# Layer 2 of a two-layer convolution kernel: its 3x3 as four quarter-array matmuls per tap, its last convolution in float32 on row halves

## The chip, the cores and the metric

The kernel runs on one core of a Trainium2 chip. Its time is the device time of one execution, in microseconds (us). Engines: TensorE (PE in the rows, PEld for its weight loads), VectorE (DVE), ScalarE (ACT), GpSimd (POOL) and SyncE (SP), which issues most of the DMAs.

## What is computed

Input x is 4 images of 1024 channels, 64x64, float32. Layer 1 is a deformable bottleneck block; layer 2 is a masked block in four groups. Cut to what matters:

```python
# layer 1
out = relu(bn(conv1x1(x, w1)))                      # 1024 -> 256
offset = conv3x3(out, w_off) + b_off                # 256 -> 18
out = deform_conv3x3(out, offset, w2)               # 4 gathered corners per tap, 9 taps, 256 -> 256
out = relu(bn(out))
x = relu(bn(conv1x1(out, w3)) + x)                  # 256 -> 1024
# layer 2, everything in G=4 groups
m1 = expand(mask, 1024); m2 = expand(mask, 256)     # one 8x8 mask per group, each cell 8x8 pixels
out = relu(gconv1x1(x * m1, w1)) * m2               # per group 256 -> 64
out = relu(gconv3x3(out, w2, pad=1)) * m2           # per group 64 -> 64
out = gconv1x1(out, w3)                             # per group 64 -> 256
return relu(out + x)
```

## The kernel before

Work goes by blocks of 8 image rows (512 pixels, one PSUM bank wide); there are NB = 32 blocks, 8 per image. Every engine walks the same list of 42 steps, written out by hand, in program order, and waits on semaphores. In step s block s is in phase A (conv1, the pixel table in HBM), block s-1 in T (offsets, coordinates), block s-8 in B (deformable 3x3), block s-9 in C (conv3, layer 2's first convolution) and block s-10 in E (layer 2's 3x3 and last convolution). Steps 10 to 31 have all phases (22 steps); steps 32 to 39 have no A (8 steps); 40 and 41 drain. Steps go in pairs inside a hardware loop: `pipeline` takes two steps a turn.

A step is cut into nine taps k = 0 to 8. Per tap, GpSimd gathers four tiles of corners (`corners`, 8 slots), ScalarE scales the first corner (`corner0`), VectorE adds the other three in 12 operations (`interpolate`), TensorE transposes the sum (`turn_val`, 8 matmuls), ScalarE copies it out rounded (`valT_copy`), VectorE makes its remainder (`valT_low`), and TensorE multiplies one tap later (`tap(k-1)`, 12 float32r matmuls). `turn_val(k)` waits for `valT_low(k-1)`. Beside each tap stand other phases' pieces, in the table `beside` of each engine. For TensorE: `conv1`, `conv3`, `gconv1`, `offconv`, and at k = 6 `gconv2(0)`, at k = 7 `gconv2(1)` and `turn_offs`, at k = 8 `gconv3(0)`, `gconv3(1)` and a chunk of the next block's `conv1`; behind the last tap the other `gconv3`.

Layer 2 in detail. Two groups make a pair: one holds partitions 0 to 63, the other 64 to 127.

- `gconv1(pair)`: 256 channels in, 64 out, column halves of the array, into psR[pair].
- `ga_mask(pair)` (VectorE): one operation into `scratch`, then one per group (64 partitions each) into `ga`. `halo_ga`: six small copies between blocks' border rows.
- SyncE then copies each group's rows, shifted by one, to the other 64 partitions (`ga<-ga`, two DMAs of 264 KB), so that one matmul takes two vertical taps: `gconv2(pair)` needs 6 matmuls for 9 taps, per group, on a column half (128 rows by 64 columns).
- `gb_mask(pair)` writes `scratch`, ScalarE's `gb_hi` and VectorE's `gb_lo` split it into a float32r high part and a remainder, stacked on the partitions.
- `gconv3(m)`, m = 0 to 7: a 128-row matmul with `gw3_hi` and a 64-row one with `gw3_lo` into psR[m % 2]; VectorE's `out_add(m)` adds y; `gconv3(m)` waits for `out_add(m-2)`. Where phase A is off a float32 matmul with the identity adds y instead, and ScalarE's `out_relu` reads PSUM.
- The next step's `conv3(0)` and `conv3(1)` write the same two banks and wait for the last `out_add`s; `y_add(0)` must follow before `conv3(2)`. On VectorE there stand between them `coordinates` (16 small operations) and four of `interpolate`.

A plain float32 matmul shows as two records in the trace, a float32r one as one.

## Time and profile before

| | |
|---|---|
| median of three runs | 3182.59 us (3177.9 to 3191.78) |
| span of the profiled execution | 3179.8 us |
| TensorE busy | 2983.4 us, 94% |
| VectorE busy | 2489.5 us, 78% |
| DMA, mean over the span | 291 GB/s |

The span is that of one execution, from first to last instruction; what lies around it is below the spread of the runs. Steps are told apart by the start of `conv3(0)`. The 21 steps between 407.4 and 2369.2 us take 93.4 us each; the eight between 2456.7 and 3102.9 us, without phase A, 80.8 us each.

### The profile page before, as it was taken

To read this page: it belongs to the slowest core of one execution; us is meant where nothing else is said; L and a number is where in the kernel's file an instruction comes from. 1 tells how busy PE (TensorE), PEld (TensorE's weight loads), DVE (VectorE), ACT (ScalarE), POOL (GpSimd) and SP (SyncE) were. 2 spreads that over 40 slices of the span, in tenths; PEclk is the share of its full clock that TensorE was granted. 3 is DMA by queue.
4 is the path that set the end of the run, shared out by engine and by line. 5 is a ranking of instruction groups with operands and counts; after the bars stand their busy time and mean duration, and the time that the engine had idled before them with its cause. 6 is when DMAs were issued, how large, how long until landed. Compare 5 with 4: busy or idle time off the path is not lost.

```text
span 3179.8 us, 44936 instructions
## 1 busy us (share of the span) xinstructions
PE 2983.4 (94%) x11296; PEld 1648.6 (52%) x11296; DVE 2489.5 (78%) x5765; ACT 1372.0 (43%) x2658; POOL 1260.6 (40%) x1160
## 2 busy tenths in 40 slices
PE   6876899999999999999999999999999999999998
PEld 3334555555555555555555555555555555555553
DVE  2117888888888888888888888878889888888882
ACT  1113444444444444444444444444445444444442
POOL 1005443444444344444344344434444444444430
PEclk9988999999999999999999999999999999999999
DMA  9888988888888888889888888888898888888872
GB/s 297 264 264 319 316 298 301 310 292 304 287 309 300 305 288 300 302 277 321 290 297 294 303 282 305 310 293 298 306 316 279 283 304 288 303 295 301 295 255 80
DMA packets 307112, 924.75 MB, mean 291 GB/s; under 512 B 34818, under 2 KB 108674, under 8 KB 298242
## 3 DMA queue, kind: packets, MB, share of 16 engines
q0 software_dynamic: 165888, 604.05, 54.2%
q1 hardware_dynamic: 122624, 251.85, 25.1%
q10 hardware_dynamic: 18432, 67.12, 5.2%
q14 instruction: 126, 1.03, 0.1%
q8 instruction: 42, 0.69, 0.1%
HBM read 747.92 MB, written 157.68 MB: 285 GB/s over the span
## 4 chain that ended last, share of the span: by engine, by line
PE 58%; DMA 15%; DVE 11%; issue 8%; POOL 3%; ACT 2%; SPq 2%; DVEq 0%; ACTq 0%; POOLq 0%
DMA corners<-corner_tables,samples_in 13%; PE psR L589 8%; PE psR L559 8%; DVE val L1037 7%; PE psD L539 6%; PE psD L540 6%; PE psD L541 6%; PE psA L451 6%; PE psV L520 6%; PE psA L487 4%; POOL corners L416 2%; PE psR L572 2%; PE psR L608 2%; DMA y<-in_x 2%; SPq L381 2%
## 5 line engine op out<-in xcount | busy, mean ns | idle before, releaser
L416 POOL DMA_INDIRECT corners<-corner_tables,samples_in x1152 | 1246.4, 1082 | 1815.5 <-DVE val L1037 1325.7
L1037 DVE SCALAR_TENSOR_TENSOR val<-corners,samples_in,val 128x256 f32<-128x256 f32 x3456 | 1427.5, 478 | 210.1 <-ACT val L738 188.9
L738 ACT ACTIVATE val<-corners,samples_in 128x256 f32<-128x256 f32 x1152 | 519.0, 503 | 356.3 <-DMA corners<-corner_tables,samples_in 349.6
L752 ACT ACTIVATE valT_hi<-psV 128x512 fp32r<-128x512 f32 x576 | 311.6, 592 | 801.2 <-PE psD L541 633.7
L559 PE MATMUL psR<-deformed,w_sb 128*128 128x512 f32 x1024 | 488.5, 621 | 51.0 <-DVE y L938 47.5
L539 PE MATMUL psD<-valT_hi,w_hi 128*128 128x512 f32 x1152 | 488.7, 424 | 0.7 <-DVE valT_lo L1047 0.7
L1047 DVE TENSOR_TENSOR valT_lo<-psV,valT_hi 128x512 fp32r<-128x512 f32 x576 | 369.9, 683 | 146.3 <-ACT valT_hi L752 145.5
L540 PE MATMUL psD<-valT_hi,w_lo 128*128 128x512 f32 x1152 | 459.0, 398 | 0.0
L541 PE MATMUL psD<-valT_lo,w_hi 128*128 128x512 f32 x1152 | 458.5, 398 | 0.0
L520 PEld LDWEIGHTS psV<-const_sb,val 128*128 128x128 f32 x2304 | 268.8, 144 | 235.0 <-issue 119.0
L520 PE MATMUL psV<-const_sb,val 128*128 128x128 f32 x2304 | 316.2, 280 | 70.4 <-DVE valT_lo L1047 65.0
L451 PE MATMUL psA<-x_sb,w_sb 128*128 128x512 f32 x768 | 358.7, 606 | 11.0 <-DMA x_sb<-in_x 10.7
L589 PE MATMUL psR<-ga,gw_sb 128*64 128x512 f32 x1536 | 345.0, 598 | 9.7 <-DVE ga L977 8.9
L559 PEld LDWEIGHTS psR<-deformed,w_sb 128*128 128x128 f32 x1024 | 197.8, 199 | 278.1 <-issue 202.4
L771 ACT ACTIVATE y<-y,bn_shift 128x512 f32<-128x512 f32 x256 | 179.5, 720 | 263.5 <-DVE y L938 263.5
L541 PEld LDWEIGHTS psD<-valT_lo,w_hi 128*128 128x128 f32 x1152 | 218.9, 190 | 54.0
L539 PEld LDWEIGHTS psD<-valT_hi,w_hi 128*128 128x128 f32 x1152 | 220.7, 192 | 49.3 <-issue 7.9
L540 PEld LDWEIGHTS psD<-valT_hi,w_lo 128*128 128x128 f32 x1152 | 220.7, 192 | 41.8 <-issue 1.9
L451 PEld LDWEIGHTS psA<-x_sb,w_sb 128*128 128x128 f32 x768 | 141.4, 191 | 162.3 <-issue 145.5
L589 PEld LDWEIGHTS psR<-ga,gw_sb 128*64 128x64 f32 x1536 | 106.9, 136 | 217.3 <-issue 213.1
L938 DVE SCALAR_TENSOR_TENSOR y<-psR,bn_scale,y 128x512 f32<-128x512 f32 x256 | 189.4, 742 | 30.0 <-PE psR L559 30.0
L451 PE MATMUL psA<-y,w_sb 128*128 128x512 f32 x256 | 123.4, 635 | 38.9 <-DMA y<-in_x 23.7
(84 smaller groups left out, 2048.4 us busy)
## 6 DMA issues: line engine op xcount, KB each, us to landing
corner_tables<-x_sb SPq DMA_DIRECT2D x256, 256.0 KB
y<-in_x SPq DMA_DIRECT2D x128, 512.0 KB, 7.5
out<-y ACTq DMA_DIRECT2D x128, 512.0 KB, 6.7
x_sb<-in_x SPq DMA_DIRECT2D x48, 1024.0 KB, 9.0
corners<-corner_tables,samples_in POOLq DMA_INDIRECT x1152, 6.2
corner_tables<-corners SPq DMA_DIRECT2D x8, 2244.5 KB, 14.1
ga<-ga SPq DMA_DIRECT2D x64, 264.0 KB, 5.7
y<-in_x SPq DMA_DIRECT2D x8, 2048.0 KB, 11.1
```

Source lines behind the costliest of these rows:

```text
L416: nc.gpsimd.indirect_dma_start(corners[:, slot, :], None, table, bass.IndirectOffsetOnAxis(ap=index[:, TAPS * t + k:TAPS * t + k + 1], axi ...
L451: mm = pe.matmul(psA[m][:], w1_sb[:, half * KC // 2 + k, m * P:(m + 1) * P], y[:, bpar, half * KC // 2 + k, :] if blow < LAG_B else x_sb[: ...
L520: mm = pe.transpose(psV[m][:, tile * P:(tile + 1) * P], val[:, (par + k) % 2, tile, m * P:(m + 1) * P], ident)
L539: pe.matmul(psD[o][:], w2_hi[:, m, k, chunk], valT_hi[:, m, :], start=first, stop=False)
L540: pe.matmul(psD[o][:], w2_lo[:, m, k, chunk], valT_hi[:, m, :], start=False, stop=False)
L541: mm = pe.matmul(psD[o][:], w2_hi[:, m, k, chunk], valT_lo[:, m, :], start=False, stop=last)
L559: mm = pe.matmul(psR[m % 2][:], w3_sb[:, k, m * P:(m + 1) * P], deformed[:, k, :], start=k == 0, stop=k == MC - 1)
L589: mm = pe.matmul(psR[pair][64 * g:64 * g + 64, :], gw2_sb[:, 2 * pair + g, j, :], ga[:, par, 2 * pair + g, row:row + ROWS, j % 3:j % 3 + IMG],
L738: nc.scalar.activation(val[:, (bpar + k) % 2, tile, :], corners[:, n % GS, 0:CMID], ACT.Copy, scale=samples_in[:, bpar, w:w + 1]).then_inc ...
L752: nc.scalar.activation(valT_hi[:, m, :], psV[m][:], ACT.Copy).then_inc(valT_ready, 1)
L1037: nc.vector.scalar_tensor_tensor(acc, corners[:, n % GS, corner * CMID:(corner + 1) * CMID], samples_in[:, bpar, w:w + 1], acc, ALU.mult, ...
L1047: nc.vector.tensor_tensor(valT_lo[:, m, :], psV[m][:], valT_hi[:, m, :].bitcast(F32), ALU.subtract).then_inc(valT_rest, 1)
```

## The change

The four groups are laid out so that a pair's two groups are "halves" (partitions 0 to 63 and 64 to 127 of `ga`) and each half has two "slots". The host reorders the channel chunks (`CHUNKS`) for that. `gconv2` takes the nine taps one by one; each tap is four float32 matmuls of 64 rows by 64 columns, each on its own quarter of the array: rows by half, columns by slot, into psR[half]. Taps 0 to 4 stand at k = 6, taps 5 to 8 at k = 7. The DMA copies, their wait on SyncE, `gb_hi`, `gb_lo` and the split of the weights are gone: `gb_mask` writes `gb` directly (both after the second corner of k = 7), and `gconv3(i)`, i = 0 to 3, is two plain float32 matmuls of 64 rows by 128 columns, one per row half, into the two banks; it waits for both `out_add`s before it. `ga_mask` and `halo_ga` work on 128 partitions at once.

```diff
-N_D = 12
-D_MASKED = 6
-D_BOTTOM = 10
+N_D = 6
+D_MASKED = 4
+D_BOTTOM = 5
+CHUNKS = [0, 2, 1, 3, 4, 6, 5, 7]
...
-                    for own, other, g in ((0, 64, 0), (64, 0, 1)):
-                        src, dst = (ga[q:q + 64, 1 - par].rearrange("p (pair g) r x -> p g pair (r x)", g=2)[:, g]
-                                    for q in (own, other))
-                        row = IMG + 2
-                        sp.dma_start(dst[:, :, 0:ROWS * row], src[:, :, row:(ROWS + 1) * row]
-                                     ).then_inc(ga_copied, 16)
...
-                    pe.wait_ge(ga_copied, 32 * (e + 1))
-                    for j in range(6):
-                        row = 0 if j < 3 else 2
-                        for g in range(2):
-                            mm = pe.matmul(psR[pair][64 * g:64 * g + 64, :], gw2_sb[:, 2 * pair + g, j, :],
-                                           ga[:, par, 2 * pair + g, row:row + ROWS, j % 3:j % 3 + IMG],
-                                           start=j == 0, stop=j == 5)
+                    for j in taps:
+                        ky, kx = j // 3, j % 3
+                        for half in range(2):
+                            rows = slice(64 * half, 64 * half + 64)
+                            for slot in range(2):
+                                mm = pe.matmul(psR[half][64 * slot:64 * slot + 64, :], gw2_sb[rows, slot, j, :],
+                                               ga[rows, par, slot, ky:ky + ROWS, kx:kx + IMG],
+                                               start=j == 0, stop=j == TAPS - 1)
+                            if j == TAPS - 1:
+                                mm.then_inc(g2_done, 1)
...
-                    pe.matmul(psR[m % 2][:], gw3_hi[:, 2 * pair + g, chunk], gb[:, 2 * pair + g, :],
-                              start=True, stop=False)
-                    mm = pe.matmul(psR[m % 2][:], gw3_lo[own, pair, chunk], gb[own, 2 * pair + g, :],
-                                   start=False, stop="A" in on)
+                    if i == 0:
                         pe.wait_ge(gb_ready, 2 * (e + 1))
+                    else:
+                        pe.wait_ge(out_sum if "A" in on else out_ready, KC * e + 2 * i)
+                    for half in range(2):
+                        rows = slice(64 * half, 64 * half + 64)
+                        mm = pe.matmul(psR[half][:], gw3_sb[rows, bank, chunk], gb[rows, bank, :],
+                                       start=True, stop="A" in on)
...
-                    6: each(gconv2, 0),
-                    7: each(gconv2, 1) + [turn_offs],
-                    8: each(gconv3, 0, 1) + [lambda: conv1(0, 0, ahead=1, chunks=[0])],
+                    6: each(gconv2, range(0, 5)),
+                    7: each(gconv2, range(5, TAPS)) + [turn_offs],
+                    8: each(gconv3, 0) + [lambda: conv1(0, 0, ahead=1, chunks=[0])],
...
-                    after = {6: each(gb_hi, 0), 7: each(gb_hi, 1)}
+                    after = {}
...
-                    beside[6] += c1[6] + c2[6] + c3[6] + each(gb_mask, 0)
-                    beside[7] += each(gb_lo, 0) + c1[7] + c2[7] + each(gb_mask, 1) + c3[7]
-                    beside[8] += each(gb_lo, 1) + each(out_add, 0, 1) + [positions] + c1[8] + each(
+                    beside[6] += c1[6] + c2[6] + c3[6]
+                    beside[7] += c1[7] + c2[7] + each(gb_mask, 0, 1) + c3[7]
+                    beside[8] += each(out_add, 0, 1) + [positions] + c1[8] + each(
```

On TensorE, at k = 8 of a step with all phases, from behind `tap(6)` to `turn_val(8)`: `gconv3`, a chunk of the next block's `conv1` (L451), the transposes. A float32 matmul counts once here. Before:

```order
L541 MATMUL psD<-valT_lo,w_hi 128x512
L606 MATMUL psR<-gb,gw_hi 128x512
L608 MATMUL psR<-gb,gw_lo 128x512
L606 MATMUL psR<-gb,gw_hi 128x512
L608 MATMUL psR<-gb,gw_lo 128x512
L451 MATMUL psA<-x_sb,w_sb 128x512
L520 MATMUL psV<-const_sb,val 128x128 x8
```

Now:

```order
L500 MATMUL psD<-valT_lo,w_hi 128x512
L567 MATMUL psR<-gb,gw_sb 128x512 x2
L410 MATMUL psA<-x_sb,w_sb 128x512
L479 MATMUL psV<-const_sb,val 128x128 x8
L498 MATMUL psD<-valT_hi,w_hi 128x512
```

Four float32r matmuls that alternate between 128 and 64 rows have become two float32 ones of 64 rows; the same happens at the other three places, and L589 x12 at k = 6 and at k = 7 becomes L550 x20 and x16.

On VectorE, from `ga_mask` at k = 5 to the end of k = 7. Before (L957, L962 `ga_mask`; L977, L984 `halo_ga`; L1037 `interpolate`; L1047 `valT_low`; L1001 `gb_mask`; L1011 `gb_lo`):

```order
L957 TENSOR_TENSOR scratch<-psR,maskx 128x512
L962 SCALAR_TENSOR_TENSOR ga<-scratch,maskx 64x8x64 x2
L957 TENSOR_TENSOR scratch<-psR,maskx 128x512
L962 SCALAR_TENSOR_TENSOR ga<-scratch,maskx 64x8x64 x2
L977 TENSOR_SCALAR ga<-ga,const_sb 64x2x66 x4
L984 TENSOR_SCALAR ga<-ga,const_sb 64x2x66 x2
L1037 SCALAR_TENSOR_TENSOR val<-corners,samples_in,val 128x256 x12
L1047 TENSOR_TENSOR valT_lo<-psV,valT_hi 128x512 x2
L1037 SCALAR_TENSOR_TENSOR val<-corners,samples_in,val 128x256 x12
L1001 SCALAR_TENSOR_TENSOR scratch<-psR,maskx 128x512
L1047 TENSOR_TENSOR valT_lo<-psV,valT_hi 128x512 x2
L1011 TENSOR_TENSOR gb<-scratch,gb 64x512 x2
```

Now:

```order
L897 TENSOR_TENSOR scratch<-psR,maskx 128x512
L900 SCALAR_TENSOR_TENSOR ga<-scratch,maskx 128x8x64
L897 TENSOR_TENSOR scratch<-psR,maskx 128x512
L900 SCALAR_TENSOR_TENSOR ga<-scratch,maskx 128x8x64
L909 TENSOR_SCALAR ga<-ga,const_sb 128x2x66
L911 TENSOR_SCALAR ga<-ga,const_sb 128x2x66
L949 SCALAR_TENSOR_TENSOR val<-corners,samples_in,val 128x256 x12
L959 TENSOR_TENSOR valT_lo<-psV,valT_hi 128x512 x2
L949 SCALAR_TENSOR_TENSOR val<-corners,samples_in,val 128x256 x12
L959 TENSOR_TENSOR valT_lo<-psV,valT_hi 128x512 x2
L949 SCALAR_TENSOR_TENSOR val<-corners,samples_in,val 128x256 x8
L924 SCALAR_TENSOR_TENSOR gb<-psR,maskx 128x512 x2
```

Six `ga` writes have become two and six halo copies two; `gb_mask` moved from the end of k = 6 and the middle of k = 7 to one place, after the eighth corner operation of k = 7.

## Rows read from the trace of the kernel before

**Rows 1.** The page: busy time and share of each engine.

```profile
PE 2983.4 (94%) x11296; PEld 1648.6 (52%) x11296; DVE 2489.5 (78%) x5765; ACT 1372.0 (43%) x2658; POOL 1260.6 (40%) x1160
```

**Rows 2.** Waits of TensorE, 407.4 to 2369.2 us: total us, times, longest.

```profile
PE psR L559 <- DVE y L938: 36.6, 8, 5.0
PE psV L520 <- DVE valT_lo L1047: 27.4, 12, 3.4
```

**Rows 3.** Stretches: length, busy us of PE, PEld, DVE, ACT, POOL; granted clock, DMA.

```profile
323.00:407.40 84.40, 75.59 (x285) 47.10 (x284) 69.69 (x169) 35.91 (x71) 39.14 (x36) 0.94 0.88 308
407.40:2369.20 1961.80, 1895.48 (x7310) 1057.93 (x7309) 1656.12 (x3817) 897.18 (x1743) 825.39 (x757) 0.98 0.87 300
2456.70:3102.90 646.20, 620.22 (x2480) 348.82 (x2481) 558.92 (x1243) 304.60 (x603) 291.28 (x278) 0.99 0.84 291
...
1532.00:1537.00 5.00, 3.88 (x5) 1.82 (x6) 5.00 (x14) 1.01 (x2) 0.36 (x1) 0.50 1.00 378
```

**Rows 4.** Timeline of TensorE in one step: start, us, what; idle before, releaser.

```profile
1524.40 3.60 PE L559 MATMUL psR<-deformed,w_sb 128*128 128x512 f32 x8
...
1533.12 6.11 PE L559 MATMUL psR<-deformed,w_sb 128*128 128x512 f32 x8 [4.25 <-DVE y L938]
...
1581.04 5.37 PE L589 MATMUL psR<-ga,gw_sb 128*64 128x512 f32 x24
1586.34 1.09 PE L520 MATMUL psV<-const_sb,val 128*128 128x128 f32 x8
1587.19 0.48 PE L539 MATMUL psD<-valT_hi,w_hi 128*128 128x512 f32 x1
```

**Rows 5.** Timeline of TensorE, 1581.0 to 1581.3 us: the first matmuls of `gconv2(0)`.

```profile
1581.04 0.65 PE L589 MATMUL psR<-ga,gw_sb 128*64 128x512 f32 x2
```

**Rows 6.** Timeline of TensorE: `turn_val(5)`; `gconv3(0)`, `(1)`; `turn_val(8)`; behind `tap(7)`.

```profile
1481.98 1.04 PE L520 MATMUL psV<-const_sb,val 128*128 128x128 f32 x8
...
1504.25 0.39 PE L606 MATMUL psR<-gb,gw_hi 128*128 128x512 f32 x1
1504.57 0.49 PE L608 MATMUL psR<-gb,gw_lo 64*128 64x512 f32 x1
...
1505.84 1.13 PE L451 MATMUL psA<-x_sb,w_sb 128*128 128x512 f32 x2
1506.81 1.04 PE L520 MATMUL psV<-const_sb,val 128*128 128x128 f32 x8
...
1510.48 1.88 PE L451 MATMUL psA<-x_sb,w_sb 128*128 128x512 f32 x4
```

**Rows 7.** Groups of VectorE by line and shape: us busy, mean ns | idle before.

```profile
L962 DVE SCALAR_TENSOR_TENSOR ga<-scratch,maskx 64x512 f32<-64x512 f32 x128 | 88.1, 689 | 4.2
...
L977 DVE TENSOR_SCALAR ga<-ga,const_sb 64x132 f32<-64x132 f32 x128 | 36.5, 285 | 6.8 <-DVE ga L962 3.4
```

**Rows 8.** Timeline of VectorE: `out_add(4)`, then the turn of the loop.

```profile
1517.55 0.69 DVE L1020 TENSOR_TENSOR y<-psR,y 128x512 f32<-128x512 f32 x1 [1.37 <-PE psR L608]
...
1530.73 1.67 DVE L1037 SCALAR_TENSOR_TENSOR val<-corners,samples_in,val 128x256 f32<-128x256 f32 x4 [5.43 <-ACT val L738]
```

**Rows 9.** Timeline of TensorE in the step without phase E, taps 5 to 8.

```profile
368.93 1.04 PE L520 MATMUL psV<-const_sb,val 128*128 128x128 f32 x8
...
376.61 1.33 PE L520 MATMUL psV<-const_sb,val 128*128 128x128 f32 x8 [3.84 <-DVE valT_lo L1047]
383.63 1.16 PE L520 MATMUL psV<-const_sb,val 128*128 128x128 f32 x8 [1.17 <-DVE valT_lo L1047]
392.25 1.94 PE L520 MATMUL psV<-const_sb,val 128*128 128x128 f32 x8 [3.80 <-DVE valT_lo L1047]
```

**Rows 10.** Timeline of TensorE in the drain: the 3x3; two identity matmuls.

```profile
3124.55 12.22 PE L589 MATMUL psR<-ga,gw_sb 128*64 128x512 f32 x48 [4.15 <-DVE ga L977]
...
3162.77 1.13 PE L612 MATMUL psR<-y,const_sb 128*128 128x512 f32 x2
3164.49 1.12 PE L612 MATMUL psR<-y,const_sb 128*128 128x512 f32 x2
```

More of the change, by code:

```diff
@@ L573, in gconv1, with gconv2 @@
                                            y[:, odd, chunk, :], start=k == 0, stop=k == 1)
                     mm.then_inc(g1_done, 1)
[L576 removed]
+                def gconv2(taps):
                     if "E" not in on:
                         return
[L581 to L592 removed]
@@ L594, in gconv3 @@
-                def gconv3(m):
+                    if taps[0] == 0:
+                        pe.wait_ge(ga_steps, N_D * (e + 1) + D_BOTTOM if "C" in on else N_D * NB + 1)
+                        if "C" not in on:
+                            pe.wait_ge(out_ready, KC * e)
+                        pe.sem_inc(pe_waits, 1)
+                    for j in taps:
[8 more added lines that the diff above has]
+                                mm.then_inc(g2_done, 1)
@@ L610, in gconv3 @@
+                    for half in range(2):
+                        rows = slice(64 * half, 64 * half + 64)
+                        mm = pe.matmul(psR[half][:], gw3_sb[rows, bank, chunk], gb[rows, bank, :],
+                                       start=True, stop="A" in on)
+                        if "A" in on:
+                            mm.then_inc(g3_done, 1)
                     if "A" not in on:
-                        mm = pe.matmul(psR[m % 2][:], ident, y[:, par, m, :], start=False, stop=True)
@@ L613, in gconv3 @@
-                    mm.then_inc(g3_done, 1)
+                        for half in range(2):
+                            pe.matmul(psR[half][:], ident, y[:, par, 2 * i + half, :], start=False, stop=True
+                                      ).then_inc(g3_done, 1)
                 beside = {
@@ L631, in step @@
                     4: each(gconv1, 0, 1) + each(offconv, 0),
-                    5: each(gconv2, 0) + each(offconv, 1),
-                    6: each(gconv2, 1),
-                    7: each(gconv3, 0, 1) + [turn_offs],
-                    8: each(gconv3, 2, 3),
+                    5: each(gconv2, range(0, 5)) + each(offconv, 1),
+                    6: each(gconv2, range(5, TAPS)),
+                    7: each(gconv3, 0) + [turn_offs],
+                    8: each(gconv3, 1),
                 }
@@ L772, in y_relu @@
                                          bias=bn_shift[:, 4 + m:5 + m]).then_inc(y_ready, 1)
-                def gb_hi(pair):
-                    if "E" not in on:
-                        return
-                    act.wait_ge(gb_ready, 2 * e + pair + 1)
-                    if low > LAG_E:
-                        act.wait_ge(g3_done, KC * e)
-                    for g in range(2):
-                        own = slice(64 * g, 64 * g + 64)
-                        nc.scalar.activation(gb[own, 2 * pair + g, :], scratch[own, :], ACT.Copy
-                                             ).then_inc(gb_high, 1)
                 def out_relu(m):
@@ L818, in step @@
                         3: each(y_relu, 6, 7),
-                        5: [offs_copy] + each(gb_hi, 0),
-                        6: each(gb_hi, 1),
+                        5: [offs_copy],
                         8: each(out_relu, 4, 5),
@@ L959, in ga_mask @@
[L959 to L964 removed]
+                    else:
+                        dve.wait_ge(ga_steps, N_D * c + 2)
@@ L968, in halo_ga @@
                     if "C" in on:
+                        flag = inner[:, bass.ds(c, 1)]
                         dve.wait_ge(ga_steps, N_D * c + D_MASKED)
[L972 to L980 removed]
@@ L981, in halo_ga @@
-                    for g in range(2):
-                        own = ga[64 * g:64 * g + 64].rearrange("p a (pair g) r x -> p a g r pair x", g=2)[:, :, g]
-                        if "C" in on:
-                            nc.vector.tensor_scalar(own[:, odd, 0], own[:, par, ROWS],
-                                                    inner[64 * g:64 * g + 64, bass.ds(c, 1)],
-                                                    None, ALU.mult).then_inc(ga_steps, 1)
-                def gb_mask(pair):
+                        nc.vector.tensor_scalar(ga[:, par, :, ROWS + 1], ga[:, odd, :, 1], flag, None, ALU.mult
+                                                ).then_inc(ga_steps, 1)
@@ L1000, in gb_mask @@
-                    rows = lambda a: a.rearrange("p (r x) -> p r x", r=ROWS)
-                    nc.vector.scalar_tensor_tensor(rows(scratch[:]), rows(psR[pair][:]), 0.0,
-                                                   mask_rows(par, pair), ALU.max, ALU.mult).then_inc(gb_ready, 1)
-                def gb_lo(pair):
-                    if "E" not in on:
-                        return
-                    for g in range(2):
-                        own, other = slice(64 * g, 64 * g + 64), slice(64 - 64 * g, 128 - 64 * g)
-                        dve.wait_ge(gb_high, 4 * e + 2 * pair + g + 1)
-                        nc.vector.tensor_tensor(gb[other, 2 * pair + g, :], scratch[own, :],
-                                                gb[own, 2 * pair + g, :].bitcast(F32), ALU.subtract
-                                                ).then_inc(gb_rest, 1)
+                    dve.wait_ge(g2_done, 2 * e + bank + 1)
```

169 lines of the change are left out of this document (60 added, 109 removed).

## Prediction, made before the changed kernel ran

> **What bounds the kernel now.** The page's busy shares come first: TensorE 94%, VectorE 78% [rows 1]. The stretches show that this holds in the steady part: TensorE 1895.48 us of 1961.80, the DMA engines 0.87 busy [rows 3]. TensorE's waits there come to 36.6 us for `y_add` (conv3) and 27.4 for `valT_low` (`turn_val`), 3.1 us of a step's 93.4 [rows 2]. So TensorE paces most taps, and something else does at two places. One is the turn of the loop, every second step: VectorE is idle 5.43 us behind `coordinates` [rows 8], conv3 waits 4.25 us for `y_add(0)`, and its next eight records take 6.11 us instead of 3.60 at a granted clock of 0.50, the 1.2 GHz level [rows 3, 4]. The other is k = 2 of the other steps, where gathers come late behind the loads of x and y. The change touches neither, so what TensorE saves just ahead of them is lost. What it saves at k = 6 and 7 is kept if VectorE and the gathers can follow.
>
> **TensorE, the 3x3.** Four full-size float32 matmuls (eight records) are 3.60 us with the end of the last, some 3.43 from start to start: 0.43 a record [rows 4]. In `gconv2(0)`, 24 records on column halves go from 1581.04 to 1586.34, 5.30 us [rows 4]: twelve rounds of two records are 5.16, entering and leaving 0.14. Two records of some 0.64 us each lie within 0.65 [rows 5], so both halves start together. Both calls: 10.6 us. Now there are 9 taps x 4 matmuls x 2 records = 72. With all four quarters at once that is 18 rounds of 0.43 = 7.75 us, with two entries and exits 8.0: **2.6 us less** a step. No row shows row halves running together. The bounds are four at a time (-2.6) and two, 36 rounds, 15.5 us (+5.0). I take the first: the column halves reach their full factor, and the rate that it needs, a weight load and a matmul every 0.107 us, was held by `turn_val`, eight pairs from 1586.34 to 1587.19 [rows 4].
>
> A rule of the Trainium skill speaks against it. The page "TensorE: Matmul & The Clock Gate" (Part 3, The mechanism) has matmuls start and end in strict program order, and weight loads overlap only with matmuls of another row group. If the two records of a float32 matmul stand one behind the other in that order, only two quarters could run at once: the sum would be +5.0 us instead of -2.6. The trace disagrees for column halves: two records start together from the first round on, 24 take twelve rounds and not thirteen, and their weight loads are hidden though they share their rows.
>
> **TensorE, the last convolution.** `gconv3(0)` and `(1)` go from 1504.25 to 1505.84, 1.59 us for four float32r records, though the first takes 0.32 only [rows 6]; the 64-row ones cost a change of shape of 0.1 to 0.2 us each way. Four such places: 6.4 us. Now each place is two row halves of two records: 2 x 0.43 and 0.2 for the shape, 1.06, if the halves run together, 1.92 if not. Four places: 4.2 or 7.7 us, -2.1 or +1.3. I take -2.1: 0.5 at k = 8, 1.6 behind the last tap.
>
> **What of it stays.** Let X be the end of `tap(7)`, 1510.48 [rows 6]. Ahead of X the saving is 2.6 + 0.5 = 3.1 us. Behind X VectorE paces: `out_add(4)` to `(7)`, `coordinates`, four corner operations and `y_add(0)` are the same as before, and start when `gconv3` has delivered for `out_add(4)`. That was at 1517.55, X + 7.1 [rows 8]; now two conv1 chunks (1.72), `gconv3(1)` (1.06), `tap(8)` (2.8) and `gconv3(2)` (1.06) with 0.15 of latency make X + 6.8. So 0.3 of the 1.6 us stays. Where the loop doesn't turn, the late gathers of k = 2 have the same effect. A steady step saves 3.4 us less 0.1 for small misfits (the transposes of k = 8 meet `valT_low(7)` with nothing to spare): **3.3 us** (2.0 to 4.5). 22 steps: **73 us**.
>
> Does VectorE keep up? `ga_mask` loses two operations of 0.69 and the halo four of 0.285 [rows 7], so `valT_low(5)` comes 2.5 us earlier, and `turn_val(6)` only 0.8: ten rounds and the entries are 4.5 us where 5.3 were, and no wait stands there now [rows 4]. The two `gb_mask`s (0.7 each) end about 3.1 us behind `turn_val(7)`, and TensorE reaches `gconv3(0)` 3.8 behind it. `gb_hi` and `gb_lo` go without a saving of their own: VectorE's and ScalarE's work is under TensorE's at k = 7 and 8. If that cover were gone, the 2.8 us of `gb_lo` would be a gain, not a loss.
>
> **Queues.** SyncE loses two DMAs and the wait for `ga`. Behind that wait stood the next step's first load of x; it now goes when the pixel table has landed. 0.53 MB go of some 28 a step (300 GB/s x 93.4 us) [rows 3]: the rest in 3.5% less time keeps the DMA engines at 0.88. The mask load doubles from 8 to 16 KB. Taken as nothing; if the earlier load of x delays the gathers of k = 6 to 8, that is rival b.
>
> **Steps without phase A**, 80.8 us each [rows 3]. The 3x3 saves 2.6 us and some 1 us of waits for `ga`. A place of `gconv3` with its identity takes twice 1.72 us [rows 10], now 0.86 + 1.72 + 0.2 = 2.8: 2.6 for four places; its waits for two `out_relu`s are mostly hidden by a tap. Up to 6.2 us; but VectorE then has 7.5 us of work in taps of 6.6, so I take **4.5** (2.5 to 6.2). 8 steps: **36 us**. In the drain the wait of 4.15 us shortens by 2.3 and the two 3x3 take 2.6 less each [rows 10]; each of its two blocks pays 1.6 for both `gb_mask`s and 0.8 for unhidden `out_relu`s, so -2.7. The step without phase E gains 2 us from shorter `ga_mask`s, the prologue 1.5 from one weight split and half a MB of loads less.
>
> Sum: 73 + 36 + 2.7 + 2 + 1.5 = 115 us. The span was 3179.8, the median 3182.59; the difference is within the runs' spread, and I take the sum off the median: **3067 us**. A measurement of this kernel tells 0.5%, 16 us, from no change.
>
> **Rivals.**
> (a) *Never more than two quarters at a time.* For it: no row has 64-row matmuls side by side. Against it: the column halves. A step gets +5.0 and +1.3 on TensorE; ahead of X 5.0 + 0.3 count, behind it the waits swallow the rest: 5.3 x 22 = 117; without phase A 5.5 x 8 = 44; drain 8. Slower, **3350 us**. It decides from 0.157 us a record upwards (72 records 11.3 us, 0.7 more than now, which `gconv3` would still give back); four at a time need 0.107.
> (b) *Gathers or VectorE set a floor.* The step without phase E has 17 us less on TensorE and still took 84.40, only 9 less, with waits of 3.84, 1.17 and 3.80 us ahead of `turn_val(6)` to `(8)` [rows 3, 9]. From `turn_val(5)` to `(8)` it took 23.3 us (368.93 to 392.25); a full step takes 24.8 (1481.98 to 1506.81) [rows 6, 9], and my sum needs 21.7. Against it: the first of the waits stood behind `ga_mask`, now cheaper. With 23.3 as the floor a step saves 1.8: 40 + 18 + 6 = 64 us, **3119 us**.
> (c) *All four run, but below full pace*, held by the issue of two instructions every 0.107 us. At 0.13 us a record the 3x3 takes 9.6 us and saves 1.0: 115 - 1.6 x 32 = 64, again **3119 us**.
> (d) *Nothing comes of it*: all that TensorE saves returns as waits at the turn of the loop and at k = 2. The step of rival b shows half of it returning, not all. **3183 us**, within 16.
>
> **Chances.** Forecast 0.57 (3025 to 3100), b and c together 0.20 (3100 to 3160), d 0.07, a 0.13 (3330 to 3370), below 3025 0.03 (all bounds good: 4.5 x 22 + 6.2 x 8 + 6 = 155, 3028). The range of 3015 to 3160 leaves out a and d alone, 0.20. Faster by over 0.5%: 0.57 + 0.20 + 0.03 = 0.80; within: 0.07; slower: 0.13.
>
> **What will show it.** In the timeline after: the 40 records of the 3x3 at k = 6 in about 4.3 us (8.6 under a, 5.2 under c); a place of the last convolution in 1.06 (1.9 under a); `turn_val(5)` to `(8)` in 21.7 us, without a wait (under b 23.3, with waits for `valT_low` or `gb_mask`). The wait of conv3 at the turn of the loop should grow from 4.25 to about 5.4 us, the one at k = 2 by 1. `ga_mask` on 128 partitions should take the 0.69 us that 64 take now. I am wrong if row halves don't share the array, or if those waits grow by more than TensorE saves.

## The result, and the profile after

The changed kernel takes 3091.86 us (median of 4, 3088.16 to 3100.9) against 3182.81 us: ratio 0.9719, 95% interval 0.9695 to 0.9743. That is 91 us saved, where 115 were forecast. The profiled execution has a span of 3087.4 us, 92.4 less than before.

The page's shares first, the row that answers to [rows 1]; under it two rows of the chain that ended last.

```profile
PE 2848.4 (92%) x12064; PEld 1568.1 (51%) x12064; DVE 2312.3 (75%) x5439; ACT 1294.4 (42%) x2530; POOL 1240.7 (40%) x1160
...
PE 60%; DMA 15%; DVE 9%; issue 7%; POOL 3%; ACT 2%; SPq 2%; DVEq 0%; ACTq 0%; POOLq 0%
DMA corners<-corner_tables,samples_in 13%; PE psR L518 9%; PE psD L498 7%; PE psD L500 7%; PE psD L499 7%; PE psA L410 6%; PE psR L550 6%; PE psV L479 6%; DVE val L949 5%; PE psA L446 4%; PE psR L531 4%; PE psR L567 3%; POOL corners L375 3%; DMA y<-in_x 2%; SPq L340 2%
```

TensorE has 135 us less to do, but its share fell from 94% to 92%: about 43 us of what it saved came back as idle time. The chain's costliest link is not an engine at all but the gathers of the corners, 13% of the span. It had 13% of the chain of the kernel before too, and my prediction uses no row of that view:

```profile
DMA corners<-corner_tables,samples_in 13%; PE psR L589 8%; PE psR L559 8%; DVE val L1037 7%; PE psD L539 6%; PE psD L540 6%; PE psD L541 6%; PE psA L451 6%; PE psV L520 6%; PE psA L487 4%; POOL corners L416 2%; PE psR L572 2%; PE psR L608 2%; DMA y<-in_x 2%; SPq L381 2%
```

The stretches, as [rows 3] (length, busy us of PE, PEld, DVE, ACT and POOL, granted clock, DMA share, GB/s): the step without phase E, the 21 steady steps, the 8 steps without phase A.

```profile
324.70:403.20 78.50, 73.11 (x286) 44.96 (x285) 67.10 (x164) 35.86 (x71) 37.76 (x36) 0.98 0.89 324
403.20:2296.70 1893.50, 1805.85 (x7814) 1000.20 (x7813) 1537.46 (x3604) 844.48 (x1659) 788.35 (x756) 0.98 0.86 304
2385.80:3016.20 630.40, 584.42 (x2673) 330.88 (x2673) 518.20 (x1163) 287.38 (x571) 314.29 (x278) 0.99 0.83 291
```

A steady step went from 93.4 to 90.2 us (3.25 less, 3.3 forecast), a step without A from 80.8 to 78.8 (2.0 less, 4.5 forecast). In those, TensorE lost 36 us of work (620.22 to 584.42) and the stretch only 16.

TensorE's timeline in a steady step: `turn_val(7)` (L479), `gconv2` (L550) at k = 7, `gconv3` (L567) and conv1 (L410) at k = 8. These answer to [rows 4, 6].

```profile
1361.63 1.09 PE L479 MATMUL psV<-const_sb,val 128*128 128x128 f32 x8
...
1365.45 3.66 PE L550 MATMUL psR<-ga,gw_sb 64*64 64x512 f32 x32
...
1373.20 1.13 PE L567 MATMUL psR<-gb,gw_sb 64*128 64x512 f32 x4
1374.26 1.12 PE L410 MATMUL psA<-x_sb,w_sb 128*128 128x512 f32 x2
```

The 32 records take 3.66 us and the 40 of k = 6 take 4.52 (their row stands with e2_half_outer): the eight more cost 0.86 us, 0.107 us a record, all four quarters at full pace. A place of the last convolution is 1.06 us from start to start. `turn_val(5)` to `(8)` is 21.8 us in 20 of the 21 steady steps (24.8 before, 21.7 forecast).

TensorE at the turn of the loop, as [rows 4], and VectorE there, as [rows 8]. Then TensorE's waits in the steady stretch, as [rows 2].

```profile
1490.27 6.28 PE L518 MATMUL psR<-deformed,w_sb 128*128 128x512 f32 x8 [4.80 <-DVE y L880]
```

```profile
1482.29 0.26 DVE L856 TENSOR_SCALAR samples<-scratch,const_sb 128x36 int32<-128x36 f32 x1
1487.88 1.67 DVE L949 SCALAR_TENSOR_TENSOR val<-corners,samples_in,val 128x256 f32<-128x256 f32 x4 [5.33 <-issue]
1489.47 0.75 DVE L880 SCALAR_TENSOR_TENSOR y<-psR,bn_scale,y 128x512 f32<-128x512 f32 x1
```

```profile
PE psR L518 <- DVE y L880: 43.1, 17, 5.5
PE psV L479 <- DVE valT_lo L959: 34.9, 24, 3.1
```

Both waits grew, from 36.6 and 27.4 us. The larger growth is in the steps without A. TensorE's waits there, of the kernel before (2456.7 to 3102.9 us) and of the changed one (2385.8 to 3016.2):

```profile
PE psR L559 <- DVE y L938: 10.9, 15, 2.2
PE psV L520 <- DVE valT_lo L1047: 5.2, 7, 0.7
PE psR L589 <- DVE ga L977: 4.8, 7, 1.2
PE psR L572 <- ACT y L771: 4.5, 8, 0.6
PE psR L559 <- ACT y L792: 3.5, 2, 2.9
```

```profile
PE psR L531 <- ACT y L728: 14.6, 8, 1.9
PE psR L567 <- DVE gb L924: 10.9, 8, 2.1
PE psR L518 <- ACT y L737: 9.0, 7, 2.9
PE psR L518 <- DVE y L880: 7.9, 12, 2.4
PE psR L567 <- ACT y L737: 6.2, 6, 1.5
```

These five sum to 29 us before and 49 after, with three suspects: `gconv1(0)` waits for a ReLU of y, `gconv3` for `gb_mask` and `out_relu`, conv3 for `out_relu`. Behind the last two may stand ScalarE, whose copies of the first corner wait for gathers (e3_ring12 tests it). ScalarE's row for that, before and after, in the same stretches:

```profile
ACT val L738 <- DMA corners<-corner_tables,samples_in: 74.7, 62, 4.5
```

```profile
ACT val L695 <- DMA corners<-corner_tables,samples_in: 89.1, 88, 2.9
```

### The profile page after: what moved, and what is told of

Same layout as the page of the kernel before. It is cut to its first block, busy times and chain, and to the rows that moved or that the text cites. A ratio compares the mean times of both kernels' runs of the same rounds, so it can differ in the third digit from the quotient of the medians.

```text
span 3087.4 us, 45424 instructions
## 1 busy us (share of the span) xinstructions
PE 2848.4 (92%) x12064; PEld 1568.1 (51%) x12064; DVE 2312.3 (75%) x5439; ACT 1294.4 (42%) x2530; POOL 1240.7 (40%) x1160
## 4 chain that ended last, share of the span: by engine, by line
PE 60%; DMA 15%; DVE 9%; issue 7%; POOL 3%; ACT 2%; SPq 2%; DVEq 0%; ACTq 0%; POOLq 0%
DMA corners<-corner_tables,samples_in 13%; PE psR L518 9%; PE psD L498 7%; PE psD L500 7%; PE psD L499 7%; PE psA L410 6%; PE psR L550 6%; PE psV L479 6%; DVE val L949 5%; PE psA L446 4%; PE psR L531 4%; PE psR L567 3%; POOL corners L375 3%; DMA y<-in_x 2%; SPq L340 2%
## 5 line engine op out<-in xcount | busy, mean ns | idle before, releaser
L375 POOL DMA_INDIRECT corners<-corner_tables,samples_in x1152 | 1228.7, 1067 | 1750.1 <-DVE val L949 1257.6
L695 ACT ACTIVATE val<-corners,samples_in 128x256 f32<-128x256 f32 x1152 | 522.1, 505 | 396.2 <-DMA corners<-corner_tables,samples_in 390.0
L479 PEld LDWEIGHTS psV<-const_sb,val 128*128 128x128 f32 x2304 | 266.2, 143 | 237.0 <-issue 131.4
L479 PE MATMUL psV<-const_sb,val 128*128 128x128 f32 x2304 | 313.4, 279 | 69.9 <-DVE valT_lo L959 64.9
L410 PE MATMUL psA<-x_sb,w_sb 128*128 128x512 f32 x768 | 357.8, 605 | 12.6 <-DMA x_sb<-in_x 12.6
L550 PE MATMUL psR<-ga,gw_sb 64*64 64x512 f32 x2304 | 261.5, 594 | 2.7 <-DVE ga L909 1.9
L410 PEld LDWEIGHTS psA<-x_sb,w_sb 128*128 128x128 f32 x768 | 141.1, 191 | 196.5 <-issue 178.0
L567 PE MATMUL psR<-gb,gw_sb 64*128 64x512 f32 x512 | 144.9, 642 | 33.0 <-DVE gb L924 14.7
L410 PE MATMUL psA<-y,w_sb 128*128 128x512 f32 x256 | 125.9, 646 | 37.5 <-DMA y<-in_x 24.5
```

Of the source, the lines that this page charges most:

```text
L375: nc.gpsimd.indirect_dma_start(corners[:, slot, :], None, table, bass.IndirectOffsetOnAxis(ap=index[:, TAPS * t + k:TAPS * t + k + 1], axi ...
L410: mm = pe.matmul(psA[m][:], w1_sb[:, half * KC // 2 + k, m * P:(m + 1) * P], y[:, bpar, half * KC // 2 + k, :] if blow < LAG_B else x_sb[: ...
L479: mm = pe.transpose(psV[m][:, tile * P:(tile + 1) * P], val[:, (par + k) % 2, tile, m * P:(m + 1) * P], ident)
L550: mm = pe.matmul(psR[half][64 * slot:64 * slot + 64, :], gw2_sb[rows, slot, j, :], ga[rows, par, slot, ky:ky + ROWS, kx:kx + IMG], start=j ...
L695: nc.scalar.activation(val[:, (bpar + k) % 2, tile, :], corners[:, n % GS, 0:CMID], ACT.Copy, scale=samples_in[:, bpar, w:w + 1]).then_inc ...
```

## The experiments

All ten are read against this table: distances between the first records of conv3 of successive steps, in us of one profiled execution each. Where two kernels run the same steps, the entries tell how far one execution can be trusted: e4_tail_gconv1 and the changed kernel differ by 0.5 us in the 21 steady steps, but by 4.3 in the front. "Front" is all ahead of the first of them, "no E" the step without phase E, "last A" the last step with phase A, "rest" what lies behind the eight steps without A.

| kernel | front | no E | 21 steady | last A | 8 without A | rest | median |
|---|---|---|---|---|---|---|---|
| before | 323.0 | 84.5 | 1961.7 | 87.5 | 646.2 | 76.9 | 3182.8 |
| changed | 324.7 | 78.5 | 1893.5 | 89.2 | 630.4 | 71.2 | 3091.9 |
| e1_halves | 322.8 | 80.5 | 1940.4 | 89.9 | 632.6 | 75.2 | 3142.0 |
| e2_half_outer | 323.1 | 79.2 | 1967.0 | 91.3 | 646.2 | 78.9 | 3187.2 |
| e3_ring12 | 315.4 | 75.8 | 1843.9 | 82.2 | 594.4 | 73.0 | 2988.4 |
| e4_tail_gconv1 | 320.4 | 78.8 | 1893.0 | 89.6 | 661.0 | 71.2 | 3116.9 |
| f1_before_ring12 | 320.1 | 80.2 | 1917.5 | 84.5 | 628.8 | 76.5 | 3108.5 |
| f2_copies_back | 326.5 | 82.4 | 1910.6 | 87.3 | 629.5 | 71.3 | 3109.1 |
| f3_gconv3_unpaired | 322.2 | 78.6 | 1910.8 | 89.1 | 645.7 | 78.2 | 3124.4 |
| f4_ring12_gconv1_order | 314.5 | 77.3 | 1845.4 | 82.2 | 586.3 | 71.2 | 2975.6 |
| f5_ring12_unrolled | 311.3 | 75.8 | 1802.8 | 82.2 | 592.4 | 71.3 | 2941.8 |
| g1_ring12_no_loop | 309.5 | 77.2 | 1789.4 | 82.2 | 592.4 | 73.3 | 2925.7 |

### The 3x3 in its old form: does TensorE's saving reach the end?

```
-                    for j in taps:
+                    bank = 0 if taps[0] == 0 else 1
+                    for j in range(6):
...
-                        for half in range(2):
-                            rows = slice(64 * half, 64 * half + 64)
-                            for slot in range(2):
-                                mm = pe.matmul(psR[half][64 * slot:64 * slot + 64, :], gw2_sb[rows, slot, j, :],
+                        for slot in range(2):
+                            mm = pe.matmul(psR[bank][64 * slot:64 * slot + 64, :], gw2_sb[:, slot, j, :],
```

> The changed kernel, but the 3x3's matmuls in the form of the kernel before: per call six taps as two column halves with all 128 rows (12 float32 matmuls, 24 records, two calls a step), everything else as changed. It takes the wrong taps and sums, so the 3x3's part of the output is not the reference's; only its cost counts. My theory, TensorE sets the pace at k = 6 and 7: the places of the 3x3 go from 8.0 back to 10.6 us a step, 2.6 x 22 = 57 us where phase A runs, 10 to 20 in the steps without A, 5 in the drain: 3160 to 3175 us. Rival, the gain came from the cheaper masking or from the DMAs that are gone, and TensorE's time there is hidden: under half of that, below 3130 us.

Measured: 3141.96 us, ratio 0.9876 [0.9859, 0.9894], 50 us more than the changed kernel. The 3x3 is 5.37 us a call again:

```profile
1379.85 5.37 PE L549 MATMUL psR<-ga,gw_sb 128*64 128x512 f32 x24
```

The steady steps pay 46.9 us, 2.2 of the 2.6 each. The eight steps without A pay 2.2 us together, of the 10 to 20 I had expected: there TensorE got 2.6 us a step more to do and a step grew by 0.3. So the theory holds where A runs, and it falls in the last steps, where something else sets the pace. The 3x3 explains some 50 of the 91 us. The copies' removal will account for some 17 more (f2_copies_back), and the rest, some 24, no run takes apart: the last convolution's new form, the cheaper masking and the missing `gb_hi` and `gb_lo` are in it.

### Row halves far apart in the program

```
-                    for j in taps:
-                        ky, kx = j // 3, j % 3
-                        for half in range(2):
-                            rows = slice(64 * half, 64 * half + 64)
+                    for half in range(2):
+                        rows = slice(64 * half, 64 * half + 64)
+                        for j in taps:
+                            ky, kx = j // 3, j % 3
```

> The changed kernel with the two loops of the 3x3 exchanged: all taps of a call on row half 0 first, then all on row half 1, so that instructions of different row halves stand 10 to 20 records apart instead of 4. Same matmuls, same result. Theory 1, the four quarters overlap only where they stand close behind each other in TensorE's order, so that this form runs two quarters at a time: the 3x3 takes 72 records x 0.107 x 2 = 15.4 us instead of 8.0 (somewhat less where the halves meet), +7 us a step, about +150 us where A runs and +30 to 50 without: 3260 to 3290 us. This is then also the price of my rival a. Theory 2, a row half of the array runs on whatever the order is, since its instructions wait in a queue of their own: 3092 us, within 10.

Measured: 3187.22 us, ratio 1.0016 [0.9999, 1.0032]. The whole gain of the change is gone, though the matmuls are the same. The 40 records of k = 6, here and in the changed kernel:

```profile
1578.90 7.15 PE L550 MATMUL psR<-ga,gw_sb 64*64 64x512 f32 x40
```

```profile
1357.17 4.52 PE L550 MATMUL psR<-ga,gw_sb 64*64 64x512 f32 x40
```

One row half at a time would be 20 rounds of 0.43 us, 8.6 and 0.15 for entry and exit. 7.15 us is about four rounds less, and the records' starts show which: two at a time every 0.43 us up to 1581.10, four at a time from 1581.53 to 1582.82, two at a time again from 1583.31. So the second half's first record starts beside the seventh of the first half's ten rounds, ahead of six records that stand before it in the program, and no earlier. In all 60 calls that stand alone (30 of 40 records, 30 of 32) exactly four rounds run together. Theory 1's mechanism holds, with a boundary of four rounds, but not its price; theory 2 is out. The calls of the 3x3 take 12.4 us a step where I had put 15.4. This is a milder form of rival a in my prediction, and its measured price: 95 us above the changed kernel, level with the kernel before.

### Twelve slots for the gathers

```
-GS = 8
+GS = 12
```

> The changed kernel with 12 slots for gathered corners instead of 8, so that gathers are issued one tap further ahead. Theory 1, in the steps without A the late gathers hold ScalarE and VectorE, and through them gb_mask and out_relu, and at k = 2 of every second step they hold TensorE for 2 to 3 us: waits of ScalarE's corner copies on the DMA of the corners (0.5 to 1.8 us each) go, 2 us a step in the steps without A and 1 in the others: 3092 - 16 - 22 = 3054 us. Theory 2, the order of ScalarE's and VectorE's own work makes these waits and the gathers only happen to end last: 3092 us within 8.

Measured: 2988.44 us, ratio 0.9395 [0.9382, 0.9408]: 103 us less than the changed kernel, where theory 1 had hoped for 38. One number gives more than the whole change did. The chain that ended last loses the gathers:

```profile
PE 82%; DVE 7%; issue 4%; DMA 4%; SPq 2%; ACT 1%; POOL 1%; DVEq 0%; ACTq 0%; POOLq 0%
PE psR L518 12%; PE psA L410 11%; PE psD L498 9%; PE psD L500 9%; PE psD L499 9%; PE psR L550 9%; PE psV L479 8%; PE psA L446 4%; PE psR L567 4%; PE psR L531 4%; DVE val L949 3%; PE psR L573 3%; DMA y<-in_x 2%; SPq L340 2%; DVE y L932 1%
```

TensorE's waits in the steady stretch (391.2 to 2235.1 us), then those of the eight steps without A:

```profile
PE psR L518 <- DVE y L880: 41.5, 17, 5.4
PE psR L567 <- DVE y L932: 6.7, 21, 0.3
PE psV L479 <- DVE valT_lo L959: 2.6, 12, 0.3
```

```profile
PE psR L531 <- ACT y L728: 14.6, 8, 1.9
PE psR L518 <- ACT y L737: 1.9, 1, 1.9
PE psR L518 <- DVE y L880: 1.1, 2, 0.6
PE psR L567 <- DVE gb L924: 0.5, 1, 0.5
```

The wait for `valT_low` at k = 2 is gone (34.9 to 2.6), and so are those for `gb_mask` and `out_relu`. Three are left: the turn of the loop, `gconv1(0)`, and the short ones for `out_add`. A step without A is 72.8 to 74.6 us now, where the changed kernel has 78.8 on average. That the number of slots does it is shown; why eight are too few is argued from rows. POOL's group row says 1067 ns for one gather of four, and it lands 5.9 us after its issue (median of the DMA view), so the last of a tap's four lands some 4 x 1.07 + 5.9 = 10 us after the slot of the first came free (an estimate from these two). With 8 slots that must fit into little more than one tap, and most taps of these steps are 6.6 to 9.3 us long (from one `turn_val` to the next); with 12 there is another tap of room.

```profile
L375 POOL DMA_INDIRECT corners<-corner_tables,samples_in x1152 | 1228.7, 1067 | 1750.1 <-DVE val L949 1257.6
...
L695 ACT ACTIVATE val<-corners,samples_in 128x256 f32<-128x256 f32 x1152 | 522.1, 505 | 396.2 <-DMA corners<-corner_tables,samples_in 390.0
```

ScalarE's 390.0 us of waits for the gathers (above, the changed kernel) are 38.4 with 12 slots.

### The kernel before with twelve slots

```
-GS = 8
+GS = 12
...
-        w2_lo = sb("w2_lo", [P, MC, TAPS, CMID], F32R)
+        w2_lo = w2_hi
...
-                                                by_block(w2_hi[:])[:, i:j].bitcast(F32), ALU.subtract
+                                                by_block(w2_hi[:])[:, i:j].bitcast(F32), ALU.max
```

> The kernel before with 12 slots for gathered corners. To make room, the low parts of the 3x3 deformable weights share the tile of the high parts (the step that forms them writes a maximum there): same instructions, same sizes, the low part of these weights is left out of the result. It gives the value of the change where no gather is late. Theory 1, the part of my forecast that didn't come (115 us forecast, 91 measured) was eaten by late gathers: the change is then worth at least the forecast, and this kernel takes the 2988 us of the changed one with 12 slots + 115 = 3103 us, up to 3120. Theory 2, the change is worth its 91 us whatever the gathers do: 3079 us.

Measured: 3108.46 us, ratio 0.9755 [0.9736, 0.9773]. Against e3_ring12 the change is worth 120 us, as theory 1 said (115 to 132), and not 91. Stretch by stretch it saves 4.7, 4.4, 73.6, 2.3, 34.4 and 3.5 us. My terms were 1.5, 2, 73 for the 22 steps with phases A and E (73.6 + 2.3 here), 36 and 2.7. So the sum comes near, 115 for 120, where the gathers are in time; the kernel on record had other waits.

### The copies of `ga` put back

```
+                if "C" in on:
+                    sp.wait_ge(ga_steps, N_D * (s - LAG_C) + D_MASKED)
+                    sp.sem_inc(sp_waits, 1)
...
+                        sp.dma_start(dst[:, :, 0:ROWS * row], src[:, :, row:(ROWS + 1) * row]
+                                     ).then_inc(ga_copied[1 - par], 16)
```

> The changed kernel (8 slots) with the two copies of ga a step put back, 264 KB each, at the place in SyncE's order where they stood, into a tile that nothing reads; only the masking two steps later waits for them. They contribute nothing to the result. Theory 1, the copies cost nothing and their removal gave nothing: 3092 us, within 10. Theory 2, late gathers set the pace in the short steps, so anything that adds traffic or stands in SyncE's queue adds to them: some 0.5 to 1 us a step, 3107 to 3125 us.

Measured: 3109.13 us, ratio 0.9761 [0.9735, 0.9787], 17 us more than the changed kernel. The two intervals overlap by a little, but the table shows where the time went: 17.1 us in the steady steps, where the changed kernel and e4_tail_gconv1 differ by 0.5, and 3.9 in the step without E; nothing in the eight without A, where I had expected most. So theory 2 has the size right and the place wrong. ScalarE's waits for gathers went from 390.0 to 440.4 us:

```profile
ACT val L708 <- DMA corners<-corner_tables,samples_in: 440.4, 315, 17.1
```

So two DMAs that had hardly ever held TensorE were worth 0.8 us a steady step, most likely through the gathers. Whether by their bytes or by their place in SyncE's queue ahead of the next load of x, no run tells.

### The last convolution without pairs

```
-                        mm = pe.matmul(psR[half][:], gw3_sb[rows, bank, chunk], gb[rows, bank, :],
+                        mm = pe.matmul(psR[half][:], gw3_sb[:, bank, chunk], gb[:, bank, :],
```

> The changed kernel with both matmuls of each place of the last convolution on all 128 rows instead of one on each row half; the sums are then over both halves, so that this part of the result is not the reference's. They should no longer run beside each other: a place takes 4 records x 0.43 = 1.7 us plus the change of shape instead of 1.06, +0.85 x 4 = 3.4 us a step. If TensorE paces all of them: 3.4 x 32 = 109, 3200 us. I expect less, since the two or three places behind the end of the last tap only lengthen what VectorE and ScalarE wait for there and shorten the wait at the turn of the loop: 50 to 90 us, 3140 to 3180. Rival, the last convolution is hidden behind out_add and out_relu: under 20 us.

Measured: 3124.37 us, ratio 0.9807 [0.9789, 0.9826], 33 us more. A place is 1.98 us instead of 1.13, the 0.85 more that I had worked out:

```profile
1559.42 1.98 PE L567 MATMUL psR<-gb,gw_sb 128*128 128x512 f32 x4 [0.26 <-DVE gb L924]
```

TensorE's busy time in the steady stretch grew by 37.5 us (1805.85 to 1843.35), 1.8 a step and not 3.4; a step pays 0.8 of it, and a step without A 1.9. The total lies between my 50 to 90 and the rival's 20, so that I had put it too high. In the steady stretch waits get shorter: conv3's from 43.1 to 40.1 us, `turn_val`'s from 34.9 to 26.0, `gconv3`'s for `out_add` from 6.7 to none. The 0.8 is about what the one place ahead of X costs, and that fits the little, 0.3 of 1.6 us, that the prediction let stay behind X.

### `gconv1` one place later in the last steps

```
-                    4: each(gconv1, 0, 1) + each(offconv, 0),
+                    4: each(offconv, 0),
...
                     turn_val(k)
+                    if k == 4 and "A" not in on:
+                        gconv1(0)
+                        gconv1(1)
                     tap(k - 1)
```

> The changed kernel; in the 8 steps without A both gconv1 stand behind turn_val(4) instead of ahead of it. Theory: there gconv1(0) waits 1.8 us a step for the ReLU of chunk 7 (0.5 before), since its four chunks are now 0, 2, 4, 6 of the new order and the wait is for chunk 6's ReLU plus one; one turn_val later (about 1.5 us of other work ahead of it) most of this wait is covered: 8 x 1.3 = 10 us less, 3082 us. Rival: the masking that follows on VectorE, and gb_mask behind it, come later by as much, and TensorE waits there: 3092 us or some us more.

Measured: 3116.94 us, ratio 0.9797 [0.9779, 0.9814]: 25 us slower than the changed kernel, all of it in the eight steps (661.0 us instead of 630.4). TensorE, then VectorE, in one of them:

```profile
2582.20 1.34 PE L479 MATMUL psV<-const_sb,val 128*128 128x128 f32 x8 [2.69 <-DVE valT_lo L962]
2583.47 5.21 PE L531 MATMUL psR<-y,gw_sb 128*64 128x512 f32 x16
```

```profile
2587.01 0.69 DVE L900 TENSOR_TENSOR scratch<-psR,maskx 128x512 f32<-128x512 f32 x1 [4.27 <-PE psR L531]
```

The wait for the ReLU went, and TensorE waited 2.69 us for `valT_low(3)` instead. Then `ga_mask` stood in VectorE's order ahead of the corners of the next tap, with nothing to do for 4.27 us: the rival, at a far higher price than I gave it. The 16 records behind the wait also took 5.21 us instead of 3.65, at a granted clock of 0.69 (2583.4 to 2588.6 us). Before work is moved behind a wait, look at what the other engines have queued behind its result.

### The order of the chunks in `gconv1`

```
-                    pe.wait_ge(y_ready, KC * c + 7 + slot)
+                    pe.wait_ge(y_ready, KC * c + 6 + 2 * slot)
...
-                            chunk = 4 * half + 2 * k + slot
+                            chunk = 4 * half + k + 2 * slot
```

> The changed kernel with 12 slots, with gconv1(0) on the places 0, 1, 4 and 5 of y and gconv1(1) on 2, 3, 6 and 7, as the chunks stood before the change, so that gconv1(0) waits for the sixth ReLU and not for the seventh (the y_add it waits for stays the seventh, because of the bank). The weights and the chunks no longer fit together, so this part of the result is not the reference's. Theory: the 1.8 us wait of gconv1(0) for ScalarE's ReLU in each of the 8 steps without A comes from the new order of the chunks alone: 8 x 1.3 to 1.8 = 10 to 14 us less than 2988, 2975 us. Rival: the wait is really for the seventh y_add, or moves to gconv1(1), whose ReLU is 0.9 us later: 2988 us, within 4.

Measured: 2975.59 us, ratio 0.9351 [0.9334, 0.9368], 13 us less than with 12 slots alone. The eight steps without A go from 594.4 to 586.3 us; the row of the wait, 14.6 us before, is now

```profile
PE psR L531 <- ACT y L728: 4.5, 8, 0.6
```

and the kernel before had 4.5 us there too. The new order of the chunks makes `gconv1(0)` wait for the seventh ReLU instead of the sixth, and costs 8 to 13 us. My prediction doesn't mention it. This kernel prices the wait and is no version to keep; I didn't look for an order that keeps both.

### The turns of the loop

```
-                    with eng.Fori(s // 2, end // 2) as pair:
-                        for par in range(2):
-                            step(2 * pair + par, par, on[par], s + par)
+                    many = 6 if (end - s) % 6 == 0 else end - s
+                    if end - s == many:
+                        for i in range(many):
+                            step(s + i, i % 2, on[i % 2], s + i)
+                    else:
+                        with eng.Fori(s // many, end // many) as group:
+                            for i in range(many):
+                                step(many * group + i, i % 2, on[i % 2], s + i)
```

> The changed kernel with 12 slots, and with its main loop turned 2 times instead of 8 (six steps in a turn instead of two) and the two short loops written out. Same work in the same order. Theory 1, the wait of conv3 for y_add (4.0 to 5.4 us, and 1.5 of conv1 or turn_val ahead of it) in every second step is there only because VectorE starts a new turn of the loop: each turn that goes gives 6 to 7 us, 8 of 10 turns go: 2988 - 52 = 2936 us. Theory 2, VectorE pays per new code rather than per turn, and written-out steps pay in each place: 2988 us or more.

Measured: 2941.75 us, ratio 0.9241 [0.9225, 0.9256], 47 us less than e3_ring12. Nearly all its steady steps are 85.0 to 85.4 us; the two at a turn are 6.1 and 4.5 longer. VectorE where e3_ring12 still turned its loop, behind the same instruction as in the rows of the result:

```profile
814.16 0.26 DVE L861 TENSOR_SCALAR samples<-scratch,const_sb 128x36 int32<-128x36 f32 x1
814.31 1.67 DVE L954 SCALAR_TENSOR_TENSOR val<-corners,samples_in,val 128x256 f32<-128x256 f32 x4
815.89 0.74 DVE L885 SCALAR_TENSOR_TENSOR y<-psR,bn_scale,y 128x512 f32<-128x512 f32 x1
```

5.33 us of idle time became none. A profile can mislead here: VectorE stood idle for 4.6 to 6.0 us at all eight turns of e3_ring12, and its rows put that down to ScalarE's `val` (L695). But in f5_ring12_unrolled VectorE's operation starts at 814.31, ahead of the ScalarE operation that stands at the same place, so it never needed that one:

```profile
817.91 1.70 ACT L700 ACTIVATE val<-corners,samples_in 128x256 f32<-128x256 f32 x4
```

All engines' loops were written out together. That VectorE's turn is the costly one is read from its idle time; TensorE has no idle stretch of that length at a turn but its wait for `y_add`. With all loops written out (`many = end - s`):

> The changed kernel with 12 slots and with all loops written out (the one with six steps in a turn took 2942 us, with 6.2 and 4.5 us still lost at its two turns). Theory 1, a loop's turn costs VectorE its time and nothing else does: 2942 - 11 = 2931 us. Theory 2, the code that is written out is fetched late in some places: 2942 us or more.

Measured: 2925.73 us, ratio 0.9196 [0.9178, 0.9213]. All 21 steady steps but the first take 85.2 to 85.3 us. The steady stretch and the page's first row:

```profile
386.70:2176.10 1789.40, 1776.87 (x7814) 988.53 (x7813) 1534.25 (x3604) 826.14 (x1659) 795.53 (x756) 1.00 0.90 323
```

```profile
PE 2799.2 (96%) x12064; PEld 1546.0 (53%) x12064; DVE 2307.6 (79%) x5439; ACT 1262.4 (43%) x2530; POOL 1264.6 (43%) x1160
```

TensorE is busy 99% of the steady stretch at a granted clock of 1.00. This is the version to use: 166 us below the changed kernel and 257 below the one before. Theory 1 had 2931 us, 5 too many.

## Why the prediction was right, and where it wasn't

**TensorE's terms** held. The 3x3 runs its four quarters at 0.107 us a record: 8.0 us where 10.6 were. A place of the last convolution takes 1.06. `ga_mask` on 128 partitions takes 694 ns, where 64 took 689 [rows 7]. Rivals a and c are out for the form in which the change writes the loop. A milder rival a is e2_half_outer: with another order of the same loops nothing is left of the gain.

The rule of the Trainium skill that I had set against the change ("TensorE: Matmul & The Clock Gate", Part 3, The mechanism: matmuls start and end in strict program order) would have made it 5.0 us slower a step if taken with two records to a matmul. The trace decides against that reading: 72 records in 8.0 us. In e2_half_outer a row half that stands far behind in the order mostly waits its turn, but even there it starts ahead of six earlier records, so the order of starts isn't strict between row halves.

**"A steady step saves 3.3"** came out as 3.25, but partly by luck. The removal of the copies, "taken as nothing", gave 0.8 us of it (f2_copies_back, 17.1 over 21 steps). Without late gathers a steady step saves 3.5 (73.6 over 21). The wait at the turn of the loop grew by half of what I had said: from 4.25 to 4.80 us in the step shown and from 4.6 to 5.1 in the mean of the eight, where 5.4 was forecast. The wait at k = 2 was to grow by 1 us and grew by 0.4 (2.3 to 2.7 in the mean); beside it conv3 and `turn_val` at k = 0 and 1 now wait 0.3 and 0.2 us.

**"Steps without phase A: 4.5 us"** is the term that was mis-sized: 36 us forecast, 15.8 measured, and that is most of the 24 us missing. I had bounded it by VectorE's work, "7.5 us of work in taps of 6.6". VectorE wasn't it: with 12 slots the same instructions save 4.3 us a step, and the taps that the 6.6 stands for are 6.6 to 6.7 us long in e3_ring12. The failing step is in the paragraph on the queues, where the gathers were made a rival for k = 6 to 8 only, instead of being timed against the shortest taps. Two rows of the trace before pointed at the gathers: the chain with 13% for them, and ScalarE's 74.7 us of waits for them in these steps. Neither tells that these steps would pay, since ScalarE waited as long in a steady step, 10.0 us for 9.3:

```profile
ACT val L738 <- DMA corners<-corner_tables,samples_in: 209.9, 150, 4.5
```

It took the run with 12 slots to tell. A second part is the new order of the chunks in `gconv1`, some 1.3 us a step, which the diff showed and the sum left out.

**"Its waits for two out_relus are mostly hidden"** was wrong: `gconv3` and conv3 wait 6.2 and 9.0 us for them, where 3.5 were. With 12 slots 1.9 us of them are left, so they too came from late gathers; `out_relu` stands behind the corner copies in ScalarE's order.

**The rest**: the last step with A was to save 3.3 us and lost 1.7, from the same cause (2.3 saved with 12 slots). The drain gave 5.7 us and the step without E 6.0, where I had 2.7 and 2; of the 6.0, 3.9 go again when the copies are put back. The front lost 1.7 where I had 1.5 gained; two executions of the same front differ by up to 4.3 (table), so that says little. So 115 - 20 (steps without A) - 6.5 (steady and last A: 66.5 for 73) + 7 (drain and the step without E) - 3 (front) = 92. The drain and the step without E made up 7 of the 30 us that the other terms lacked, and that was luck. Rival b named the mechanism, the gathers as a floor, and gave it to the wrong steps; its 3119 us was too much.

## What to carry to other kernels

When an engine is at 94% and still waits, time the DMAs that feed its slowest neighbour against the shortest stage before costing a saving: issue and landing against the number of buffers. Here four more buffers, for which the change made room, were worth 103 us, more than the change's 91. Put the loop over the quarters of the array innermost, since row halves share it only if they stand near each other in the program, and write a loop out before tuning around the wait at its turn.

## What the runs showed of the hardware

- float32 matmuls on 64x64 quarters reach the full factor of four: 0.107 us a record of 512 columns, weight loads hidden. With all of one row half ahead of the other in the program, the last four rounds of the first ran beside the first four of the second, in all 60 calls that stand alone, and no more did (7.15 us for 40 records, against 4.52).
- VectorE stood idle for 5.33 us behind the last instruction of a loop's body (4.6 to 6.0 at the turns of e3_ring12), and for none where the next step's code simply follows. TensorE's clock then made it worse: after the 4.80 us wait eight records took 6.28 us instead of 3.60, at a granted clock of 0.57 (1490.2 to 1496.4 us), where the eight ahead of the wait had 1.00. The Trainium skill has a reason for the first ("Runtime: NRT & Kernel Launch", Instruction fetch mechanics: a taken branch out of the fetched window stops the engine until its code arrives). The runs agree with it, though no row shows code being loaded: eight turns fewer gave 47 us, two more 16. Written-out code of all engines showed no price in the steady steps, 85.2 us each.
- Half a MB of copies a step, which held TensorE for next to nothing, cost 17 us; ScalarE's waits for gathers grew by 50 us with them.
